# A graph layer's edge loop: one window of node rows for two blocks of edges, and edges laid out four blocks to a partition

## The reference, cut to what matters

```python
dst = jnp.minimum((6250 * jax.random.uniform(key, (100000,)) ** 2.0).astype(jnp.int32), 49999)
_o = jnp.argsort(dst, stable=True)                 # so dst is sorted, and denser at low nodes
src, dst = src[_o], dst[_o]

row, col = src, dst
msg_in = concatenate([x[row], x[col]])             # 256 features per edge
h = relu(msg_in @ Wm1 + bm1)
h = relu(h @ Wm2 + bm2)
messages = h @ Wm3 + bm3
agg = segment_sum(messages, col, num_nodes) / clip(count, 1)
upd = relu(concatenate([x, agg]) @ Wn1 + bn1) @ Wn2 + bn2
y = x + upd
out = layernorm(x + y)
```

## Time and profile before

| | |
|---|---|
| median of three runs | 1202.34 us |
| profiled execution, first to last instruction | 1416.6 us |
| its head, to the first transpose of a gathered row | 89.45 us |
| its loop, first transpose of block 0 to that of block 390 | 1218.5 us |
| what lies behind that | 108.6 us |
| TensorE, VectorE, ScalarE, GpSimd busy | 88%, 69%, 52%, 56% |
| granted clock of TensorE, mean | 0.993 |

### The profile page before, as it was taken

One profiled execution on the slowest core, in us unless ns is written; L12 is line 12 of the kernel. 1 busy time (PEld: TensorE's weight loads), 2 busy tenths in 40 slices (PEclk: granted clock), 3 DMA queues, 4 the chain that ended last, 5 costly groups with the idle time before them and its releaser, 6 DMA issues.

```text
span 1416.6 us, 33766 instructions
## 1 busy us (share of the span) xinstructions
PE 1249.7 (88%) x9614; PEld 1172.0 (83%) x9615; DVE 979.6 (69%) x2072; ACT 740.6 (52%) x1392; POOL 786.5 (56%) x814
## 2 busy tenths in 40 slices
PE   6978888888888888888888889988999989899997
PEld 6868888888888888888888888888888888888886
DVE  6846666766766666766766766767767767777676
ACT  3544555555555555555555555555554555545585
POOL 2166666666666666666666666666666666564000
PEclk9999999999999999999999999999999999999999
DMA  9665555545545555555545555455545454554022
GB/s 308 274 234 156 146 144 151 149 141 151 151 140 150 152 142 147 151 143 147 152 139 150 146 143 151 145 144 152 139 147 151 138 150 144 145 151 142 10 67 86
DMA packets 135605, 211.42 MB, mean 149 GB/s; under 512 B 24247, under 2 KB 102669, under 8 KB 134030
## 3 DMA queue, kind: packets, MB, share of 16 engines
q1 hardware_dynamic: 98030, 108.43, 25.3%
q0 software_dynamic: 37536, 102.55, 25.1%
HBM read 188.09 MB, written 22.80 MB: 149 GB/s over the span
## 4 chain that ended last, share of the span: by engine, by line
PE 80%; issue 12%; DVE 2%; SPq 1%; another core or an unknown queue 1%; DMA 1%; ACT 1%; DVEq 1%; ACTq 0%
PE bank L1437 39%; PE bank L1413 11%; PE bank L1324 6%; PE sums L1345 4%; PE sums L1341 4%; PE sums L1347 3%; PE sums L1349 3%; PE bank L1478 2%; PE sums L1491 1%; PE bank L1234 1%; PE bank L1219 1%; PE bank L1461 1%; PE sums L1219 1%; DMA b_win<-b_table 1%
## 5 line engine op out<-in xcount | busy, mean ns | idle before, releaser
L630 POOL DMA_INDIRECT a_edge<-a_table,src_idx x782 | 767.1, 981 | 457.8 <-remote 268.2
L1437 PE MATMUL bank<-w,h 128*128 128x256 f32 x4692 | 661.4, 283 | 104.9 <-issue 102.1
L1437 PEld LDWEIGHTS bank<-w,h 128*128 128x128 f32 x4692 | 596.5, 188 | 119.7 <-issue 118.7
L1106 DVE SCALAR_TENSOR_TENSOR h<-bank,h 128x512 fp32r<-128x512 f32 x391 | 268.7, 687 | 338.4 <-issue 326.7
L732 ACT ACTIVATE h<-bank 128x512 fp32r<-128x512 f32 x391 | 233.8, 598 | 475.3 <-remote 439.2
L721 ACT COPY bank<-b_bc 128x512 f32<-128x512 f32 x391 | 231.5, 592 | 115.2 <-issue 66.7
L1118 DVE SCALAR_TENSOR_TENSOR h_lo<-bank,h_hi 128x512 fp32r<-128x512 f32 x391 | 266.5, 681 | 0.1
L1413 PE MATMUL bank<-ident,a_edge 128*128 128x128 f32 x1564 | 237.4, 274 | 21.1 <-issue 16.6
L740 ACT ACTIVATE h_hi<-bank 128x512 fp32r<-128x512 f32 x391 | 232.6, 595 | 2.8 <-PE bank L1437 2.8
L1413 PEld LDWEIGHTS bank<-ident,a_edge 128*128 128x128 f32 x1564 | 180.3, 140 | 40.5 <-issue 34.2
L1324 PE MATMUL bank<-onehot_t,b_win 128*128 128x256 f32 x782 | 190.3, 325 | 0.0
(11 more groups left out here) (190 smaller groups left out, 682.7 us busy)
## 6 DMA issues: line engine op xcount, KB each, us to landing
b_win<-b_table SPq DMA_DIRECT2D x391, 128.0 KB
rel<-rel_dram SPq DMA_DIRECT2D x196, 128.0 KB
a_edge<-a_table,src_idx POOLq DMA_INDIRECT x782
a_table<-work SPq DMA_DIRECT2D x12, 512.0 KB, 4.6
b_table<-work SPq DMA_DIRECT2D x5, 1024.0 KB
b_table<-h SPq DMA_DIRECT2D x4, 1024.0 KB
f_x<-in_x SPq DMA_DIRECT2D x12, 256.0 KB, 5.2
b_table<-a_edge SPq DMA_DIRECT2D x3, 1024.0 KB, 5.8
```

The source lines that it names most:

```text
L630: pool.indirect_dma_start(a_edge[:, b % R * TB + t, :], None, a_table, bass.IndirectOffsetOnAxis(ap=src_idx[:, b * TB + t:b * TB + t + 1], ...
L1106: dve.scalar_tensor_tensor(h1[:, k % U, 1, :], bank[k % 2][:, :], 0.0, h1[:, k % U, 0, :].bitcast(F32), ALU.max, ALU.subtract).then_inc(s_ ...
L1437: ins = pe.matmul(to, h1[:, j, a, h * EB + t * P:h * EB + (t + 1) * P], w2[:, b, h, :], start=False, stop=(a == 1 and h == KH - 1), skip_g ...
```

## The change

Loads of B are made per pair. `b_win` has one load for two blocks, 64 nodes from the lower of the two blocks' first nodes; the numbers in `rel` and the count of further spans are taken from that same node. Only two of `b_win`'s four buffers are used, one for each pair of a body.

Edges lie four consecutive blocks to a partition: partition p holds edges 1024 p to 1024 p + 1023. So `dst` and `src` are each loaded by one DMA of 97 partitions with 4 KB and one of a single partition with the last 672 edges. The first and last nodes, and `rel`, go to device memory by one store each where there were four. The column layouts on ScalarE follow (the copies of the transposed edges write with a larger stride), VectorE has one more small operation on the edges and one more wait among the words.

```diff
-        full = E // EB
-        loads = []
-        for n in range(2):
-            for g in range(GR):
-                rows = min(full - g * BG, BG)
-                if rows:
-                    loads.append((n, g, 0, rows, EB))
-            if E % EB:
-                loads.append((n, GR - 1, rows, 1, E % EB))
+        RUN = GR * EB
+        rows, rest = E // RUN, E % RUN
+        loads = [(n, row, many, edges) for n in range(2) for row, many, edges in ((0, rows, RUN), (rows, 1, rest))]
...
-            for n, g, row, rows, edges in loads:
-                at, e0 = (n * GR + g) * EB, (g * BG + row) * EB
-                sp.dma_start(edges_in[row:row + rows, at:at + edges],
-                             (dst, src)[n][e0:e0 + rows * edges].rearrange("(b e) -> b e", e=edges)
+            for n, row, many, edges in loads:
+                at, e0 = n * RUN, row * RUN
+                sp.dma_start(edges_in[row:row + many, at:at + edges],
+                             (dst, src)[n][e0:e0 + many * edges].rearrange("(b e) -> b e", e=edges)
                              ).then_inc(s_edges, 16)
...
-                    for j in range(GR):
-                        sp.dma_start(mm_dram[j * BG:(j + 1) * BG, :], minmax_i[0:BG, 2 * j:2 * j + 2]
-                                     ).then_inc(s_scr, 16)
+                    sp.dma_start(mm_dram.rearrange("(p g) c -> p (g c)", g=GR), minmax_i[0:BG, :]
+                                 ).then_inc(s_scr, 16)
...
-                    for j in range(GR):
-                        sp.dma_start(rel_dram[j * BG:(j + 1) * BG, :],
-                                     rel16[0:BG, j * EB:(j + 1) * EB]).then_inc(s_scr_rel, 16)
+                    sp.dma_start(rel_dram.rearrange("(p g) e -> p (g e)", g=GR), rel16[0:BG, :]
+                                 ).then_inc(s_scr_rel, 16)
...
-                first = load_words(sp, words_sp, i * U, U, PAD_DST)
-                for k in range(U):
-                    if there(i, k - RB):
-                        sp.wait_ge(s_ex, i * U + (k - RB + (2 if k % 2 == 0 else 1)))
-                    if k % 2 == 0:
-                        sp.dma_start(rel[:, k // 2, :].rearrange("p (b e) -> p b e", b=2),
-                                     rel_dram[bass.ds(i * U + k, 2), :].partition_broadcast(P)
-                                     ).then_inc(s_rc[k // 2], 16)
-                    if there(i, k):
-                        sp.dma_start(b_win[:, k % RB, :].bitcast(F32),
-                                     b_table[bass.ds(first[k] * 2, P), :]).then_inc(s_bw[k % RB], 16)
+                first = load_words(sp, words_sp, i * NP, NP, PAD_DST)
+                for c in range(NP):
+                    if there(i, 2 * c - U):
+                        sp.wait_ge(s_ex, i * U + (2 * c - U + 2))
+                    sp.dma_start(rel[:, c, :].rearrange("p (b e) -> p b e", b=2),
+                                 rel_dram[bass.ds(i * U + 2 * c, 2), :].partition_broadcast(P)
+                                 ).then_inc(s_rc[c], 16)
+                    sp.dma_start(b_win[:, c, :].bitcast(F32),
+                                 b_table[bass.ds(first[c] * 2, P), :]).then_inc(s_bw[c], 16)
...
+                dve.tensor_tensor(pair_low[0:BG, :], minmax[0:BG, 0:2 * GR:4], minmax[0:BG, 2:2 * GR:4], ALU.min
+                                  ).then_inc(s_wi, 1)
...
-                dve.tensor_copy(words_sp[0:1, :], lowest).then_inc(s_rw, 1)
-                dve.tensor_tensor(far, highest, lowest, ALU.subtract).then_inc(s_rw, 1)
+                dve.tensor_tensor(words_sp[0:1, :], row_in[0:1, 0:2 * NB:4], row_in[0:1, 2:2 * NB:4], ALU.min
+                                  ).then_inc(s_rw, 1)
+                dve.wait_ge(s_rw, 2)
+                dve.tensor_tensor(by_pairs(far), by_pairs(highest), pair_lowest, ALU.subtract).then_inc(s_rw, 1)
...
-                dve.wait_ge(s_bw[k % RB], nth(i, k, 16))
+                    dve.wait_ge(s_bw[k // 2 % RC], nth(i, k, 16))
...
-                    expand(b_win[:, k % RB, :], onehot_t[:, k % 2, :], k).then_inc(s_ex, 1)
+                    expand(b_win[:, k // 2 % RC, :], onehot_t[:, k % 2, :], k).then_inc(s_ex, 1)
```

More of the change, by code:

```diff
@@ L22 @@
 RC = 2
+NP = U // 2
 AHEAD = 2
@@ L79, in gnn_layer @@
         dst_col = sb("dst_col", [P, NB * TB], F32)
-        words_sp = sb("words_sp", [1, NB], I32)
+        words_sp = sb("words_sp", [1, NB // 2], I32)
         words_act = sb("words_act", [1, NB + 2 * U], I32)
@@ L187, in gnn_layer @@
         first_start = carve(GR)
+        pair_low = carve(GR // 2)
         dst_place = carve(GR, EB).bitcast(I32)
@@ L261, in gnn_layer @@
         s_rc = [sem(f"s_rel_loaded{c}") for c in range(RC)]
-        s_bw = [sem(f"s_b_win_loaded{c}") for c in range(RB)]
+        s_bw = [sem(f"s_b_win_loaded{c}") for c in range(RC)]
         s_bf = sem("s_b_far_loaded")
@@ L443, in gnn_layer @@
         assert NW * P // QUARTER <= 256
-        full = E // EB
-        assert (GR - 1) * BG <= full
-        loads = []
-        for n in range(2):
-            for g in range(GR):
-                rows = min(full - g * BG, BG)
-                if rows:
-                    loads.append((n, g, 0, rows, EB))
-            if E % EB:
-                loads.append((n, GR - 1, rows, 1, E % EB))
+        RUN = GR * EB
+        rows, rest = E // RUN, E % RUN
+        assert BG - 1 <= rows + (rest > 0) <= BG and GR == U and rest
+        loads = [(n, row, many, edges) for n in range(2) for row, many, edges in ((0, rows, RUN), (rows, 1, rest))]
         NPAIR = pair(NG - 1, (size(NG - 1) + 1) // 2 - 1)
@@ L524, in _ @@
                     sp.wait_ge(s_rel16, 1)
[L525 to L529 removed]
+                    sp.dma_start(rel_dram.rearrange("(p g) e -> p (g e)", g=GR), rel16[0:BG, :]
+                                 ).then_inc(s_scr_rel, 16)
+            sp.wait_ge(s_scr_rel, 16)
             sp.wait_ge(s_bz, 16)
@@ L577, in _ @@
                                base=0, pattern=[[-1, P]], channel_multiplier=1).then_inc(s_const, 1)
-            pool.memset(edges_in[:, (GR - 1) * EB:GR * EB], PAD_DST).then_inc(s_pad, 1)
-            pool.memset(edges_in[:, (2 * GR - 1) * EB:2 * GR * EB], 0).then_inc(s_pad, 1)
+            pool.memset(edges_in[:, rest:RUN], PAD_DST).then_inc(s_pad, 1)
+            pool.memset(edges_in[:, RUN + rest:2 * RUN], 0).then_inc(s_pad, 1)
             pool.memset(f_x[:, NW - 1, :], 0.0).then_inc(s_xz, 1)
@@ L614, in _ @@
             pool.wait_ge(s_et, 2 * GR)
-            pool.wait_ge(s_scr_rel, 16 * GR)
+            pool.wait_ge(s_scr_rel, 16)
             pool.wait_ge(s_bz, 16)
@@ L645, in edge_columns @@
                     act.wait_ge(s_et, n * GR + g // 2 * 2 + 2)
-                    act.copy(col[:, g * BG * TB:(g + 1) * BG * TB].rearrange("p (b t) -> p t b", t=TB),
+                    act.copy(col[:, :].rearrange("p (b g t) -> p g t b", g=GR, t=TB)[:, g, :, :],
                              bank[6 + g // 2][:, g % 2 * TB * BG:(g % 2 + 1) * TB * BG]
@@ L844, in range_of_first @@
                                   ).then_inc(s_wi, 1)
-                dve.wait_ge(s_wi, 5)
+                dve.tensor_tensor(pair_low[0:BG, :], minmax[0:BG, 0:2 * GR:4], minmax[0:BG, 2:2 * GR:4], ALU.min
+                                  ).then_inc(s_wi, 1)
+                dve.wait_ge(s_wi, 6)
             def make_relative():
-                dve.tensor_tensor(rel16[0:BG, :].rearrange("p (g e) -> p g e", g=GR), dst_f,
-                                  minmax[0:BG, 0:2 * GR:2].unsqueeze(2).to_broadcast([BG, GR, EB]), ALU.subtract
+                dve.tensor_tensor(rel16[0:BG, :].rearrange("p (c e) -> p c e", c=NP),
+                                  edges_f[0:BG, 0:GR, :].rearrange("p (c g) e -> p c (g e)", c=NP),
+                                  pair_low[0:BG, :].unsqueeze(2).to_broadcast([BG, NP, 2 * EB]), ALU.subtract
                                   ).then_inc(s_rel16, 1)
@@ L886, in _, with by_pairs @@
             far = row_far[0:1, 0:NB]
+            pair_lowest = words_sp[0:1, :].unsqueeze(2).to_broadcast([1, NB // 2, 2])
+            def by_pairs(row):
+                return row.rearrange("p (c k) -> p c k", k=2)
             def ranges_and_spans():
@@ L902, in first_words @@
                 dve.wait_ge(s_rw, 6)
-                dve.scalar_tensor_tensor(words_act[0:1, 0:NB], far, float(2**13), lowest, ALU.mult, ALU.add
-                                         ).then_inc(s_rw, 1)
+                dve.scalar_tensor_tensor(by_pairs(words_act[0:1, 0:NB]), by_pairs(far), float(2**13), pair_lowest,
+                                         ALU.mult, ALU.add).then_inc(s_rw, 1)
                 dve.tensor_scalar(row_start[0:1, :], row_third[0:1, :], float(STRIDE // QUARTER), None, ALU.mult
```

2 lines of the change are left out of this document (1 added, 1 removed).

## The result

The changed kernel took 1241.09 us (median of four runs, 1239.73 to 1241.93), the kernel before 1202.9 us beside it (1200.86 to 1204.38). The ratio is 1.0315, 95% interval 1.0303 to 1.0328: 38.2 us, or 3%, slower. The forecast was 1251 us, with a range of 1233 to 1264.

What follows compares the result with a forecast made beforehand. The prediction took TensorE to set the loop's pace at 2.57 us a block, with another chain in the head. Its sum was 1202.3 + 29 + 0 + 0 + 20 = 1251 us, range 1233 to 1264.

Steps and rivals of the forecast that it cites:

- The two rules: Loop: relieving only another engine or the DMA engines returns at most about 2 us; any new TensorE wait is paid in full.
- Part 1: Head: edge loads of 97 partitions, a prime number, run on a single DMA engine, so edges land later: +29 us.
- the sign named for one engine: Head: a DMA share of 0.06 with some 25 GB/s for most of 10 to 38 us.
- Part 2: Head: four issues in place of ten and one store in place of four, twice, change nothing: 0 us.
- the shadow: Head: the saving from fewer issues lies hidden behind the late edges of Part 1, so it counts 0.
- the first rival: Head: edges spread over many engines after all; larger rows then save 0.8 us, total 1221 us; chance 0.07.
- Part 3: Loop: half of the window loads gives 0 to 2 us, taken as 0, since DMA engines are not the limit.
- Part 4: Loop's end: second windows for blocks 383, 387 and 389 stop TensorE and lower its clock: +20 us for the three.
- Spread edges: Head: the first rival, edge loads use many engines after all, total 1221 us; chance 0.07.
- Hidden windows: Loop's end: the second windows hide in ScalarE's idle time, total 1232 us; chance 0.07.
- A longer backlog: Head: the single engine also delays later stores, and tables' stores are waited for, some 10 us more, 1262 and above; chance 0.05.
- Faster: Loop: window landings set TensorE's pace, so half the loads save 2 us, with 0.8 from the head: 1199.5 us; chance 0.02.

Runs made afterwards that it cites:

- e3: The changed kernel with each 97-partition edge load split into 96 and 1, and the three second windows left out: 1204.67 us.
- e4: The kernel before with its six edge loads of 98 partitions cut into 97 and 1, all else as it was: 1226.13 us.
- e1: The changed kernel with the 97 partitions of each edge load taken as 96 and 1: 1214.12 us.
- e5: e1 with ScalarE issuing a block's first second window ahead of its step for the block before: 1214.64 us.
- e2: The changed kernel with the three second windows left out, edges still loaded as 97 partitions: 1232.07 us.

## Why the prediction was right, and which of its terms was not

**What bounds the kernel: right.** The two rules held: half the window loads gave nothing (e3 against e4), every wait of TensorE was paid. The reading that the 214 us of gaps belong to the profiled execution is borne out, as no later profile has them (that of e4, whose loop is the loop of before, spans 1224.5 us beside a run of 1226.23). By the same reading the forecast of a profiled span of 1466 was wrong: it carried the gaps over. The span is 1239.1.

**Part 1, one engine, +29 us: right in cause; the size came out near by two errors that nearly cancel.** The loss is 28.5 us by the trace, 27.0 by e1. Edges landed at 39.6 (forecast near 41), the loop began at 117.97 (near 118), and the sign named for one engine, a share of 0.06 at some 25 GB/s, is there from 14 to 24 us (0.06, 26 GB/s). But the 32 us were too short and the 2.7 us taken off them too: from the first issue to the landing the changed kernel took 39.55 - 3.15 = 36.4 us (795 KB, 21.8 GB/s over all of it, with loads of `x` and weights moving beside it at both ends), and before took 11.48 - 3.16 = 8.3. So the edges are 28.1 us late, and that this is near 29 is in part luck. One part of the mechanism I had not seen: SyncE itself stands in its issues, 15.80 us in the second pair, so the loads behind are not only slow but not yet asked for. By the trace both end together (edges 39.6, `x` of the next group 40.0); what the late issues cost by themselves is not shown by any run.

**Part 2, fewer issues, 0: right as the shadow goes.** With the shadow gone (e3) it is no gain of 0.8 us, as the first rival had it, but a loss of 2.1; that the last row and the strided copies make it is read from traces only.

**Part 3, half of the loads, 0: right.** e3 and e4, 2.574 and 2.576 us a block.

**Part 4, three second windows: right blocks, wrong size, and a path that was right only in part.** The step that failed is the 20 us: 9.8 by the trace, 9.0 and 9.5 by runs. The path first: the forecast let each stop end with a landing of `b_far`, and left VectorE out. In the changed kernel VectorE's second one-hot ends two of the three stops. Of the idle time before `b_far`'s instructions the profile gives (weight loads and matmuls together; then the matmuls that the landing ended):

```profile
  DMA b_far<-b_table: 7.1, 4
  DVE onehot_t L1031: 3.6, 2
...
  PE bank L1325: 1.4, 1
```

So of the matmuls' 5.0 us, 3.6 fall to VectorE and 1.4 to the landing. e5 shows that it counts: with the load issued early and VectorE as it was, nothing changed. Then three numbers were off.
- ScalarE's lag. I took 3.2 us from the expand to the end of ScalarE's step, and 0.5 for the word; the trace after has, from the expand's end at 1101.88 + 0.48 = 1102.36, 1103.74 - 1102.36 = 1.4 us to the issue (1.1 and 1.0 at the other two), and the issue comes while the step's last operation still runs (1103.41 to 1104.01), not behind it. The 3.2 came from the earlier trace rows, which lie in the profile with the gaps, where ScalarE ran late. In e4, which has the loop of before without the gaps, the same lag is (1113.83 + 0.59) - (1112.12 + 0.48) = 1.8 us (its rows stand below). My low end, 2.2 "ScalarE up with TensorE", was near the state of the loop, and I chose the row over it.
- The landing: 2.1, 2.6 and 2.9 us instead of 3.6, which was read from one landing at the loop's start.
- The clock: 1.7 us in each of three; it fell after one stop only, and cost 2.63 - 1.58 = 1.05 us in the second layer and 0.45 in the transposes behind it.

```profile
1112.12 0.48 PE L1326 MATMUL bank<-onehot_t,b_win 128*128 128x256 f32 x2
...
1113.83 0.59 ACT L742 ACTIVATE h_hi<-bank 128x512 fp32r<-128x512 f32 x1
```

**The rivals.** Spread edges: refuted by e1 and e4. Hidden windows: refuted by e2. A longer backlog: the store of table A was waited for 2.01 us against 2.18 before, so none. Faster: refuted by e3. The sum was some 10 us high in one term, and the time fell inside the range because the range had the low end of that term in it.

## What to carry to other kernels

Before a layout is changed, take the number of partitions of each DMA apart: by the counts above 98 or 96 used 14 or 16 engines here, 97 used one, and that alone cost 24 to 27 us in a kernel of 1202. Taking bytes off engines that are not the limit gains nothing, but a rare branch that makes the bounding engine wait costs some 3 us each time, and moving one of two producers ahead changes nothing while the other comes just as late. When a profiled execution is longer than the runs by gaps, don't take an engine's lag from its rows.

## What the runs showed of the hardware

- An issuing queue can be held up by the DMA it issues: two DMAs on one engine took 15.80 us to issue (97 x 4 KB and a short one), against 1.92 us for five on many engines.
- While loads of 97 partitions were all that moved, the DMA engines' share was 0.06 at 26 GB/s; taking one partition out of six loads of 98 made their landing 23.1 us later.
- The same window load landed 2.1 to 3.4 us after an issue behind ScalarE's step and 2.7 to 5.1 us after an earlier one. Why stays open.
- Four copies of 128 x 196 with a stride of 8 numbers in what they write took 1.57 us on ScalarE, against 1.02 us with a stride of 2.
- Stops of TensorE of about the same length don't all cost the clock. In the changed kernel the granted clock was 0.65 behind the first (1.97 us) and 1.00 behind the second (1.39 us); in e1 it stayed at 1.00 behind the first (2.02 us) and was 0.68 behind the last (2.09 us):

```profile
1079.30:1084.00 4.70, 4.54 (x35) 4.34 (x36) 2.34 (x5) 2.48 (x5) 2.52 (x3) 1.00 0.30 96
...
1100.80:1104.00 3.20, 3.03 (x16) 2.83 (x17) 1.84 (x4) 1.61 (x3) 0.00 (x0) 0.68 0.03 5
```

What decides which stop loses it stays open.
